# Batch 0's q and k parts copied straight into the stacks, Wqkv loaded in thirds, and the order of steps laid out anew

## The reference: what is computed

```python
qkv = x @ Wqkv + bqkv                       # x [8, 512, 256]
scores = einsum('bhid,bhjd->bhij', q, k) / sqrt(16) + alibi_causal_bias
out = einsum('bhij,bhjd->bhid', softmax(scores), v)
x = layernorm(x + out @ Wo + bo)
q(w) = clip(round(w / mean|w|), -1, 1) * mean|w|
x = layernorm(x + (silu(x @ q(W_up).T) * (x @ q(W_gate).T)) @ q(W_down).T)
```

## Time and profile before

| | us |
|---|---|
| median of 3 runs | 624.56 (618.70 to 626.22) |
| the profiled execution's own time | 623.43 |
| its span | 621.7 |
| TensorE busy | 583.4 |
| VectorE busy | 494.3 |
| ScalarE busy | 318.9 |
| GpSimd busy | 298.9 |

### The profile page before, as it was taken

How to read it: one execution, slowest core, us unless ns; L and a number is a source line. 1 busy time by engine, 2 the same in 40 slices (tenths; PEclk the granted TensorE clock), 3 DMA queues, 4 the chain that set the end, 5 groups by cost and what they waited for, 6 DMA issues and landing times.

```text
span 621.7 us, 13208 instructions
## 1 busy us (share of the span) xinstructions
PE 583.4 (94%) x4172; PEld 348.8 (56%) x4172; DVE 494.3 (80%) x1258; ACT 318.9 (51%) x593; POOL 298.9 (48%) x504
## 2 busy tenths in 40 slices
PE   5689888999999999999999999999999999999995
PEld 3344354664656555664656656574566646446674
DVE  5388968996799859988599877989599877993765
ACT  2129713459346644477246744476255753576262
POOL 1306695346275435465174534564264543554234
PEclk9889998999999999999999999999999999999998
DMA  5965715015452073602553063602554053700101
GB/s 152 289 178 205 212 48 164 20 38 163 120 168 59 3 236 111 161 1 97 164 164 82 1 211 114 175 7 74 163 163 108 1 187 85 205 2 3 35 1 34
DMA packets 47724, 68.49 MB, mean 110 GB/s; under 512 B 4857, under 2 KB 43641, under 8 KB 44793
## 3 DMA queue, kind: packets, MB, share of 16 engines
q1 hardware_dynamic: 47691, 68.08, 37.2%
HBM read 38.44 MB, written 29.36 MB: 109 GB/s over the span
## 4 chain that ended last, share of the span: by engine, by line
PE 75%; DVE 6%; ACT 5%; POOL 4%; DMA 4%; issue 4%; SPq 1%; POOLq 0%; DVEq 0%
PE ring L695 17%; PE max_bank L614 10%; PE acc L644 9%; PE ring L632 9%; PE acc L712 7%; PE ring L590 7%; PE ring L597 4%; ACT probs L769 4%; PE ring L668 4%; PE max_bank L617 2%; PE ring L652 2%; POOL probs L1039 1%; POOL tern_down L1082 1%; PE ring L681 1%; PE max_bank L712 1%
## 5 line engine op out<-in xcount | busy, mean ns | idle before, releaser
L769 ACT ACTIVATE probs<-ring 128x512 f32<-128x512 f32 x320 | 170.7, 606 | 47.6 <-PE ring L632 45.9
L1039 POOL TENSOR_SCALAR_AFFINE_SELECT probs<-probs 128x256 f32<-128x256 f32 (+1 forms) x320 | 120.5, 401 | 132.2 <-ACT probs L769 131.5
L893 DVE CUSTOM_DVE_ANT_0 max_bank<-max_bank,causal_wide 128x384 f32<-128x384 f32 (+1 forms) x256 | 157.2, 637 | 17.0 <-PE max_bank L614 14.5
L614 PE MATMUL max_bank<-k_stack,q_stack 112*128 112x384 bf16 (+3 forms) x512 | 131.0, 302 | 6.3 <-DVE neg_max L893 3.0
L632 PE MATMUL ring<-q_stack,k_stack 114*128 114x512 bf16 (+3 forms) x512 | 103.6, 300 | 2.9 <-DMA q_stack<-max_parts 1.4
L1075 POOL TENSOR_TENSOR hidden_lo<-hidden,hidden_hi 128x512 f16<-128x512 f32 (+1 forms) x72 | 75.1, 1049 | 63.8 <-ACT hidden_hi L800 63.5
L788 ACT ACTIVATE gating<-ring,tanh_scale 128x512 f32<-128x512 f32 (+1 forms) x72 | 45.8, 639 | 74.0 <-PE ring L695 74.0
L644 PE MATMUL acc<-probs,v_ones 128*32 128x512 f32 (+3 forms) x1024 | 79.9, 438 | 2.8 <-POOL probs L1039 2.8
L614 PEld LDWEIGHTS max_bank<-k_stack,q_stack 112*128 112x128 bf16 x512 | 50.1, 98 | 43.9 <-DVE neg_max L893 14.6
L897 DVE TENSOR_REDUCE neg_max<-max_bank 128x2 f32<-128x512 f32 (+1 forms) x96 | 63.8, 686 | 10.2 <-PE max_bank L617 8.6
L632 PEld LDWEIGHTS ring<-q_stack,k_stack 114*128 114x128 bf16 x512 | 43.8, 97 | 49.7 <-issue 18.6
(11 more groups left out here) (107 smaller groups left out, 889.7 us busy)
## 6 DMA issues: line engine op xcount, KB each, us to landing
q_stack<-qk_scratch SPq DMA_DIRECT2D x15, 768.0 KB, 6.0
k_stack<-k_slots SPq DMA_DIRECT2D x15, 768.0 KB, 7.6
qk_scratch<-qk_parts SPq DMA_DIRECT2D x16, 384.0 KB, 3.0
k_slots<-qk_parts SPq DMA_DIRECT2D x16, 384.0 KB, 2.6
xin<-x_dram SPq DMA_DIRECT2D x8, 512.0 KB, 3.5
qk_scratch<-qk_parts SPq DMA_DIRECT2D x16, 256.0 KB, 3.3
k_slots<-qk_parts SPq DMA_DIRECT2D x16, 256.0 KB, 2.3
res<-x_dram SPq DMA_DIRECT2D x8, 512.0 KB, 3.5
```

The costliest lines, as they stand in the source:

```text
L614: mm = pe.matmul(o, q_stack[0:MAX_ROW, 4 * g + h, P * tile:P * (tile + 1)], k_stack[0:MAX_ROW, 4 * g + h, 0:width], start=True, stop=tile ...
L769: rg.drained(act.activation(probs[:, g % 2, n, :], rg.bank(step)[:, :], ACT.Exp), step)
L893: dve.tensor_tensor_reduce(scores, scores, causal_wide[:, SEQ - width:SEQ], -1.0, LOWEST_START, ALU.add, ALU.min, neg_max[:, g, first_col: ...
L1039: return pool.affine_select(out=v, in_=v, compare_op=ALU.is_ge, fill=0.0, base=0, pattern=([[0, blocks]] if blocks > 1 else []) + [[1, P]] ...
```

## The change

For batch 0 alone, each slot of the stacks is set by a DMA of its own, from the 128 partitions of a part in SBUF to the 16 partitions of the slot (new function set_slots, semaphore stack_set[t], six DMAs for each t, 24 in all). SyncE issues those of q (t = 0 and 2), ScalarE those of k (t = 1 and 3), at their part_write steps. part_write and stack_read through DRAM remain for batches 1 to 7; their counts on the semaphores are one batch lower. Wqkv is loaded by three DMAs, q, k, v, with a semaphore each. bias_fold goes from PRE to FIRST, behind qk.2. All six tables are new.

```diff
-            sp.dma_start(wqkv[:, :, 0:2 * HID], w_columns[:, :, 0:2 * HID]).then_inc(weights_in[0], 16)
-            sp.dma_start(wqkv[:, :, 2 * HID:3 * HID], w_columns[:, :, 2 * HID:3 * HID]).then_inc(v_weights_in, 16)
+            for k, landed in enumerate((weights_in[0], k_weights_in, v_weights_in)):
+                cols = slice(HID * k, HID * (k + 1))
+                sp.dma_start(wqkv[:, :, cols], w_columns[:, :, cols]).then_inc(landed, 16)
...
+        def set_slots(eng, t, part):
+            stack, slots = (k_stack, K_SLOTS) if t % 2 else (q_stack, Q_SLOTS)
+            heads = slice(HEADS // 2 * (t // 2), HEADS // 2 * (t // 2 + 1))
+            for n, p in enumerate(slots):
+                if p == part:
+                    eng.dma_start(stack[DH * n:DH * (n + 1), heads, :], qk_parts[:, t, part, :]).then_inc(stack_set[t], 16)
+        def parts_free(eng, t, batch):
+            if isinstance(batch, int) and batch < 2:
+                if batch == 1:
+                    eng.wait_ge(stack_set[t], SET_DMAS)
+                return
+            eng.wait_ge(parts_written[t], PART_DMAS * (batch - 1))
...
+                        if first:
+                            set_slots(sp, t, part)
+                            continue
...
-                        if n == 0 and first and g < 2:
-                            pe.wait_ge((first_quad_in, stack_in[0])[g], STACK_DMAS)
+                        if n == 0 and first and g % 2 == 0:
+                            for t in (g, g + 1):
+                                pe.wait_ge(stack_set[t], SET_DMAS)
                             if g == 0:
+                                pe.wait_ge(consts_set, 1)
                                 pe.wait_ge(weights_in[2], 32)
...
+                    elif kind == "part_write" and first and step[1] % 2:
+                        _, t, part = step
+                        if part == HI:
+                            rg.wait_drained(act, ("qk", t))
+                        else:
+                            act.wait_ge((qk_mid_done, qk_split)[part == LO][t // 2], 2)
+                        act.sem_inc(act_passed, 1)
+                        set_slots(act, t, part)
```

More of the change, by code:

```diff
@@ L125 @@
[L125 to L129, removed]
@@ L135 @@
[L135 to L139, removed]
@@ new lines @@
+    exp.1.0 exp.1.1 exp.1.2 max.3.0 exp.1.3 exp.1.4 max.3.1 exp.1.5 max.3.2 exp.1.6 take.2.10 take.3.0 exp.1.7
+    load_res mt.2 max.3.3 abs_sum.2 take.3.1 take.3.2 take.3.3 abs_sum.0 max.3.4 qk.0 take.3.4 max.3.5 exp.1.8
+    max.3.6 mt_out.2 pv.0.0 max.3.7 exp.1.9 take.3.5 qk_out.0 pv.0.1 exp.2.0 take.3.6 max.3.8 pv.0.2 take.3.7 pv.0.3
+    exp.2.1 exp.2.2 max.3.9 exp.2.3 split.0 exp.2.4 take.3.8 wsum max.3.10 pv.1.0 take.3.9 exp.2.5 part_write.0.0
+    nt.0 take.3.10 exp.2.6 mt.3 pv.1.1 exp.2.7 exp.2.8 nt_out.0 pv.1.2 qk.1 mt_out.3 exp.2.9 ternary.0 exp.3.0
@@ L142 @@
+    exp.3.1 pv.1.3 exp.3.2 qk_out.1 exp.3.3 part_write.0.1 part_write.0.2 exp.3.4 exp.3.5 pv.2.0 exp.3.6
+    part_write.1.0 exp.3.7 nt.1 ternary.1 pv.2.1 nt_out.1 exp.3.8 pv.2.2 exp.3.9 split.1 pv.2.3 nt.2 part_write.1.1
+    pv.3.0 pv.3.1 part_write.1.2 pv.3.2 ternary.2.0 nt_out.2 pv.3.3 at.0 nt.3 wo.0.0 nt_out.3 at.1 ternary.2.1
+    stack_read.0 wo.1.0 wo.0.1 ternary.2.2 wo.1.1
 """
 SECOND_ORDER = """
-    max.0.0 v.0 max.0.1 v_out.0 qk.2 take.0.0 max.0.2 max.0.3 take.0.1 take.0.2 max.0.4 max.0.5 v.1 take.0.3 max.0.6
@@ new lines @@
+    swish.7 exp.0.7 mt_out.1 swiglu.7 down.5 exp.0.8 max.3.1 take.2.10 exp.0.9 hidden_hi.7 max.3.2 exp.1.0 load_res
+    take.3.0 exp.1.1 take.3.1 max.3.3 exp.1.2 exp.1.3 max.3.4 down.6 exp.1.4 exp.1.5 max.3.5 take.3.2 mt.2 take.3.3
+    max.3.6 down.7 exp.1.6 exp.1.7 qk.0 take.3.4 exp.1.8 take.3.5 mt_out.2 max.3.7 exp.1.9 take.3.6 ffn_sum.0
+    ffn_sum.1 take.3.7 max.3.8 take.3.8 exp.2.0 qk_out.0 pv.0.0 pv.0.1 pv.0.2 pv.0.3 split.0 pv.1.0 exp.2.1 exp.2.2
+    max.3.9 max.3.10 exp.2.3 exp.2.4 exp.2.5 part_write.0.0 take.3.9 pv.1.1 exp.2.6 part_write.0.1 take.3.10 mt.3
@@ L184 @@
[L184 to L187 removed]
+    qk.2 max.0.0 max.0.1 qk.3 take.0.0 take.0.1 v.0 ln1 max.0.2 x1t.0 max.0.3 take.0.2 take.0.3 x1t.1 max.0.4
@@ new lines @@
+    part_write.3.1 mt.0 max.1.7 take.1.4 down.1 take.1.5 max.1.8 gate.5 max.1.9 v.3 v_out.3 swiglu.4 take.1.6
+    max.1.10 part_write.3.2 stack_read.1 hidden_hi.4 take.1.7 up.6 up.7 swish.5 take.1.8 max.2.0 mt_out.0 down.2
+    max.2.1 exp.0.0 exp.0.1 exp.0.2 take.1.9 swiglu.5 take.1.10 exp.0.3 max.2.2 swish.6 take.2.0 swish.7 take.2.1
+    max.2.3 take.2.2 load_next gate.6 max.2.4 exp.0.4 take.2.3 exp.0.5 swiglu.6 take.2.4 mt.1 max.2.5 hidden_hi.5
+    down.3 max.2.6 take.2.5 mt_out.1 take.2.6 exp.0.6 exp.0.7 max.2.7 gate.7 hidden_hi.6 max.2.8 exp.0.8 exp.0.9
@@ new lines @@
+    take.3.2 pv.0.3 exp.1.7 exp.1.8 mt_out.2 max.3.5 take.3.3 exp.1.9 nt.0 take.3.4 max.3.6 gate.7 exp.2.0 exp.2.1
+    max.3.7 max.3.8 take.3.5 pv.1.0 exp.2.2 exp.2.3 max.3.9 max.3.10 nt_out.0 take.3.6 swiglu.7 exp.2.4 exp.2.5
+    pv.1.1 pv.1.2 take.3.7 take.3.8 exp.2.6 take.3.9 hidden_hi.6 take.3.10 down.0 mt.3 pv.1.3 hidden_hi.7 exp.2.7
+    down.1 exp.2.8 down.2 mt_out.3 down.3 down.4 exp.2.9 exp.3.0 exp.3.1 exp.3.2 down.5 down.6 exp.3.3 exp.3.4
+    exp.3.5 exp.3.6 down.7 ffn_sum.0 exp.3.7 exp.3.8 ffn_sum.1 nt.1 exp.3.9 pv.2.0 pv.2.1 ffn_stats.0 nt_out.1
```

188 lines of the change are left out of this document (87 added, 101 removed).

## The result

The changed kernel takes 629.53 us (median of 16 runs, 627.1 to 633.3); the kernel before, run beside it, 623.37 (618.7 to 626.2). The ratio is 1.0108 with a 95% interval of 1.0087 to 1.0129: it is 6 us slower, and neither the forecast of 620 nor its range to 625 holds that. The profiled execution of the changed kernel took 629.6 us.

The account below looks back on a forecast made before the run. TensorE was busy 94% of a 621.7 us span, with the time to gain at the beginning. From 623.4 us, 2.7 for an earlier normalisation and 0.8 for the clock gave 619.9, say 620.0; range 612.5 to 625.

Parts of the forecast that it names:

- add up as I had thought: Batch 0's twelve copies at the start: two queues can write different partitions at once; taken at 200 GB/s, 7.9 us.
- the 0.5 that I had put: ScalarE's issue of one DMA at the start: taken as 0.5 us, so 3 us for six before qk.2.

## What to carry to other kernels

Before a DMA is given a shape, ask which partitions it writes, not only how many; when the order of rows is free, lay them so that every transfer is spread over the SBUF, as here over every sixth of 96 partitions. Take a rate for many transfers from many transfers, in the stretch behind the first burst, or measure them alone in a kernel of their own. And cost a late start under the new order as well as an early one: an order that gains when the data is in time may lose more than the delay when it is late (here 6.6 us became 10.5). Where a chain of waits says issue, look at the landings of the other queues before taking it for no wait.

## What the runs showed of the hardware

Twelve copies of 128 KB took 15.0 us onto 16 partitions in a row, 17.7 all onto the same 16, 9.4 onto every sixth of 96. Two queues of different engines writing different groups of 16 partitions took 16.5, so they do not add up as I had thought. A transfer behind narrow ones lands late too: wo's 256 KB took 8.0 us to land behind them, and 5.0 when they were spread. A DMA issued by ScalarE took 0.68 us of its time (4.08 for six), more than the 0.5 that I had put, and it stayed hidden behind the transfers: the sixth was issued by 17.0 and landed at 29.9.
